# A decoder layer over 32 batches on one core: the loop body laid out anew on 20 slots, with the second score pass begun in a batch's own step

## The reference, cut to what matters

```python
# 1: self-attention whose small probabilities are cut
probs = softmax(x @ x.T * 256 ** -0.5)
vac = where(probs < 0.01, probs, 0).sum(-1)
sparse = where(probs < 0.01, 0, probs); sparse /= sparse.sum(-1) + 1e-9
x1 = layernorm(x + sparse @ x + 0.01 * broadcast(vac) @ W.T)
# 2: cross-attention, 16 heads of 16
q, k, v = x1 @ Wq + bq, ctx @ Wk + bk, ctx @ Wv + bv
x2 = layernorm(x1 + softmax(mask(q @ k.T / 4)) @ v @ Wo + bo)
# 3: a mixture of 8 experts, the best 2 by softmax(x2 @ Wr)
out = layernorm(x2 + sum of the two experts' (x2 @ Wi @ Wo) by their weights)
```

## Time and profile before

| | us |
|---|---|
| median of 3 runs (lowest, highest) | 911.61 (910.69, 917.72) |
| the profiled execution's own time | 906.62 |
| its span, first to last instruction | 904.5 |
| PE busy in the span | 809.0 (89%) |
| DVE busy | 691.5 (76%) |
| ACT busy | 614.2 (68%) |
| POOL busy | 200.0 (22%) |
| mean granted clock of PE, as a share of full speed | 0.982 |

### The profile page before, as it was taken

The page is one execution under the profiler, slowest core; times in us unless marked ns, Lnnn a source line. Parts: engine busy times, 40 slices in busy tenths (PEclk is TensorE's granted clock), DMA queues, the critical chain, the costliest instruction groups (busy, mean ns, idle before and its releaser), DMA issues.

```text
span 904.5 us, 22919 instructions
## 1 busy us (share of the span) xinstructions
PE 809.0 (89%) x7288; PEld 661.4 (73%) x7288; DVE 691.5 (76%) x2652; ACT 614.2 (68%) x1449; POOL 200.0 (22%) x293
## 2 busy tenths in 40 slices
PE   2768789999999999999999999999999999999875
PEld 2657667887777777787777777788777777777654
DVE  5445578888888888888888888888888888887745
ACT  1326677777877777777777777777887777777650
POOL 1201122222122222222222222222212222221011
PEclk9779999999999999999999999999999999999998
DMA  7354443444444444434444444343444444332100
GB/s 218 91 159 106 111 114 89 108 104 109 103 110 112 107 120 105 104 97 108 102 111 113 109 113 120 92 102 101 111 107 112 109 109 120 88 89 72 25 11 10
DMA packets 91159, 92.74 MB, mean 103 GB/s; under 512 B 16848, under 2 KB 86880, under 8 KB 91040
## 3 DMA queue, kind: packets, MB, share of 16 engines
q1 hardware_dynamic: 91040, 91.28, 39.6%
HBM read 28.44 MB, written 3.90 MB: 36 GB/s over the span
## 4 chain that ended last, share of the span: by engine, by line
PE 78%; ACT 6%; DVE 5%; SPq 5%; issue 4%; DMA 2%; POOL 0%; POOLq 0%; DVEq 0%; ACTq 0%
PE psum L1123 18%; PE psum L979 10%; PE psum L993 10%; PE psum L1009 9%; PE psum L1059 8%; PE psum L1052 7%; PE psum L1041 3%; PE psum L1081 3%; SPq L413 3%; ACT psum L515 2%; ACT probsT L526 2%; SPq L427 2%; PE psum L1069 1%; PE psum L1030 1%; PE psum L1023 1%
## 5 line engine op out<-in xcount | busy, mean ns | idle before, releaser
L672 DVE CUSTOM_DVE_ANT_0 scores_left<-psum,mask_add 112x375 f32<-112x375 f32 x512 | 278.3, 545 | 98.7 <-PE psum L979 90.3
L979 PE MATMUL psum<-k_stack,q_stack 96*112 96x376 f32 x512 | 196.6, 393 | 37.3 <-DVE nmax L672 23.7
L515 ACT ACTIVATE psum<-mask_u 125x448 f32<-125x448 uint8 x384 | 206.8, 543 | 10.2
L526 ACT ACTIVATE probsT<-psum 125x448 f32<-125x448 f32 x384 | 205.5, 535 | 4.2 <-PE psum L993 2.7
L993 PE MATMUL psum<-q_stack,k_stack 97*125 97x224 f32 x768 | 146.3, 279 | 11.2 <-ACT psum L515 10.9
L979 PEld LDWEIGHTS psum<-k_stack,q_stack 96*112 96x112 f32 x512 | 90.8, 177 | 80.0 <-issue 55.0
L993 PEld LDWEIGHTS psum<-q_stack,k_stack 97*125 97x125 f32 x768 | 130.2, 189 | 22.8 <-ACT psum L515 19.6
L686 DVE SCALAR_TENSOR_TENSOR mix<-psum,gate,mix 112x256 f32<-112x256 f32 x224 | 107.6, 480 | 17.0 <-PE psum L1123 4.7
L452 POOL TENSOR_SCALAR var_eps<-moments 112x1 f32<-112x1 f32 x96 | 21.2, 220 | 436.1 <-DVE moments L756 217.2
L1123 PE MATMUL psum<-we_hi,x_hi 128*112 128x512 f32 x256 | 107.4, 419 | 3.7 <-DVE mix L686 3.7
L488 POOL TENSOR_TENSOR ctx_lo<-ctx_sb,ctx_hi 128x752 fp32r<-128x752 f32 x32 | 57.2, 1789 | 202.3 <-DVE x_cas L812 202.3
(11 more groups left out here) (122 smaller groups left out, 1544.9 us busy)
## 6 DMA issues: line engine op xcount, KB each, us to landing
k_stack<-k_hi SPq DMA_DIRECT2D x256, 93.8 KB, 2.2
q_stack<-q_hi SPq DMA_DIRECT2D x256, 56.0 KB, 2.0
ctx_sb<-in_context_T SPq DMA_DIRECT2D x32, 376.0 KB, 3.3
k_stack<-k_lo SPq DMA_DIRECT2D x128, 93.8 KB, 2.2
q_stack<-q_lo SPq DMA_DIRECT2D x128, 56.0 KB, 2.0
xT<-in_x_T SPq DMA_DIRECT2D x32, 112.0 KB, 2.1
x_sb<-in_x SPq DMA_DIRECT2D x32, 112.0 KB, 2.2
out_dram<-out_sb SPq DMA_DIRECT2D x32, 112.0 KB, 2.8
```

The lines of the kernel that those rows point to most:

```text
L515: nc.scalar.activation(psum[0:KP, ST_BANKS[i % 2], 0:4 * TOK].rearrange("p (h q) -> p h q", h=4), mask_u8[b][:, KEYS + t * TOK:KEYS + (t + ...
L526: nc.scalar.activation(probsT[:, group % 2, t, :], psum[0:KP, ST_BANKS[i % 2], 0:4 * TOK], ACT.Exp, scale=-1.0).then_inc(probs_ready, 1)
L672: nc.vector.tensor_tensor_reduce(scores_left[:, n % 2, :], psum[0:TOK, S_BANKS[n % 2], 0:KEYS], mask_add[k][:, :], 1.0, 3.0e38, ALU.add, A ...
L979: nc.tensor.matmul(psum[0:TOK, S_BANKS[n % 2], 0:KEYS_EVEN], q_stack[b][0:96, c, pair, odd, :], k_stack[b][0:96, c, pair, :], start=True, ...
```

## The change

`USES` has new slots and banks, `moe` works on batch it-2 rather than it-3, and the last iteration is 34 rather than 35. The product with Wo, the norm and `x2T` (stage `join`) now belong to the iteration of `heads`; only the logits and the gate (`gate`, a new chain of semaphores) stand with `moe`.

```diff
-USES = [("x1T", 0, "G2"), ("m0", 1, "G1"), ("aT", 1, "G0"), ("qT", 2, "G2"), ("K0", 3, "G0"), ("Wo", 4, "G1"),
-        ("Sc", 5, "G2"), ("K1", 6, "G1"), ("m1", 8, "G0"), ("mx0", 8, "G2"), ("V0", 10, "G2"), ("x2T", 10, "G1"),
-        ("PT", 11, "G0"), ("m2", 12, "G2"), ("att", 13, "G1"), ("lg", 14, "G0"), ("V1", 15, "G2"), ("oT", 15, "O"),
-        ("m3", 16, "G1"), ("mx1", 16, "G0"), ("V2", 18, "G0")]
+USES = [("x1T", 0, "G2"), ("qT", 1, "G0"), ("lg", 2, "G1"), ("Sc", 3, "G0"), ("K0", 3, "G2"), ("m0", 4, "G1"),
+        ("mx0", 7, "G0"), ("K1", 7, "G2"), ("m1", 9, "G1"), ("oT", 10, "O"), ("V0", 10, "G0"), ("PT", 11, "G2"),
+        ("aT", 12, "G0"), ("att", 13, "G2"), ("m2", 13, "G1"), ("Wo", 14, "G0"), ("mx1", 14, "S1"), ("m3", 15, "G1"),
+        ("V1", 16, "G0"), ("V2", 18, "G0"), ("x2T", 19, "G1")]
...
-          "join": (-2, ("aT", "Wo", "x2T", "lg")),
-          "moe": (-3, ("m0", "m1", "m2", "m3")),
+          "join": (-1, ("aT", "Wo", "x2T")),
+          "gate": (-2, ("lg",)),
+          "moe": (-2, ("m0", "m1", "m2", "m3")),
```

On PE the scores of a batch's heads stand two slots earlier (heads 0 to 2 in slots 17 to 19 of the iteration before, the last in slot 12), and blocks 0 to 5 stand in slots 14 to 19 of the iteration in which the batch's maxima are taken, blocks 6 to 11 in slots 0 to 5 of the next:

```diff
-                    if attn and 0 < n < HEADS - 1:
-                        scores(a, n + 1)
-                    if n >= SLOTS - 2 and active("attn", it + 1):
-                        scores(p, n - (SLOTS - 2))
-                    if heads and n < BLOCKS - 1:
-                        score_block(w, n + 1)
-                    if n == SLOTS - 1 and active("heads", it + 1):
-                        score_block(a, 0)
+                    if attn and n + 3 < HEADS:
+                        scores(a, n + 3)
+                    if n >= SLOTS - 3 and active("attn", it + 1):
+                        scores(p, n - (SLOTS - 3))
+                    if heads and n + 6 < BLOCKS:
+                        score_block(w, n + 6)
+                    if attn and n >= 14:
+                        score_block(a, n - 14)
...
-                    if heads and n >= 4 and (n - 4) % 3 == 0 and n <= 13:
-                        weigh_values((n - 4) // 3)
+                    if heads and n in (2, 6, 8):
+                        weigh_values(w, (2, 6, 8).index(n) + 1)
+                    if attn and n == SLOTS - 1:
+                        weigh_values(a, 0)
```

```diff
 for n in range(SLOTS):
+    if moe and n == 0:
+        act.wait_ge(pe_join.sem, pe_join.to("x2T", o))
...
+    if heads and n + 5 < BLOCKS:
+        exponent(w, n + 5)
+    if attn and n >= 15:
+        exponent(a, n - 15)
     if proj and n == 0:
...
-    if heads and n < BLOCKS:
-        exponent(n)
-        if n + 2 < BLOCKS:
-            lay_mask(w, n + 2)
...
+    if heads and n + 7 < BLOCKS:
+        lay_mask(w, n + 7)
+    if attn and n >= 13:
+        lay_mask(a, n - 13)
```

More of the change, by code:

```diff
@@ L264, in decoder_layer @@
         pe_steps = {stage: Chain(sem(f"pe_{stage}"), [u for u, _, _ in ALL_USES if STAGE_OF[u] == stage])
-                    for stage in ("self", "proj", "attn", "heads", "join", "moe", "weights")}
+                    for stage in ("self", "proj", "attn", "heads", "join", "gate", "moe", "weights")}
         act_steps = {stage: Chain(sem(f"act_{stage}"), names) for stage, names in (
@@ L311, in stages @@
         def stages(it):
-            return [active(stage, it) for stage in ("self", "proj", "attn", "heads", "join", "moe")]
+            return [active(stage, it) for stage in ("self", "proj", "attn", "heads", "moe")]
         def batches(at):
-            return *[shift(at, ahead) for ahead in (2, 1, 0, -1, -2, -3)], at[1] % 2
+            return *[shift(at, ahead) for ahead in (2, 1, 0, -1, -2)], at[1] % 2
         block = ctx.enter_context(nc.Block())
@@ L373, in iteration @@
             def iteration(at, it):
-                own, proj, attn, heads, join, moe = stages(it)
-                s, p, a, w, o, m, k = batches(at)
-                if heads:
-                    neg_max_to_scratch(w, 1)
+                own, proj, attn, heads, moe = stages(it)
+                s, p, a, w, o, k = batches(at)
                 if active("self", it + 1):
@@ L410, in iteration @@
                     settle(sp)
-                    for n in range(PAIRS):
-                        for third, part in enumerate((q_hi, q_hi, q_lo)):
-                            sp.dma_start(q_stack[b][32 * third:32 * third + 32, :, n, :, :].bitcast(fp32),
-                                         part[32 * n:32 * n + 32, :, :, :].bitcast(fp32))\
-                                           .then_inc(q_stacked[b][n], 16)
+                    stack_queries(0)
+                    stack_queries(1)
                 if attn:
                     neg_max_to_scratch(a, 0)
+                if proj:
+                    stack_queries(2)
+                    stack_queries(3)
+                if attn:
+                    neg_max_to_stack(a, 0)
                 if proj:
@@ L422, in iteration @@
                     settle(sp)
[L423 to L431 removed]
+                    for n in range(PAIRS - 1):
+                        stack_keys(n)
+                if attn:
+                    neg_max_to_scratch(a, 1)
+                if proj:
+                    stack_keys(PAIRS - 1)
+                if attn:
+                    neg_max_to_stack(a, 1)
                 if it == FIRST:
@@ L576, in iteration @@
-                    if proj and n == 3:
+                    if proj and n == 2:
                         act.wait_ge(pe_proj.sem, pe_proj.to("qT", p))
@@ L786, in iteration @@
-                    if n == 10 and moe:
+                        if moe:
+                            dve.wait_ge(dve_gate.sem, dve_gate.to("gate_b", o))
+                            nc.vector.tensor_tensor(
+                                gate[k][:, :], gate_a[:, :], gate_b[:, :], ALU.add)\
+                              .then_inc(dve_gate.did("gate"), 1)
+                    if n == 8 and moe:
+                        expert(0)
+                        expert(1)
+                    if n == 9 and proj:
+                        low_keys(1)
```

508 lines of the change are left out of this document (252 added, 256 removed).

## The result

The changed kernel takes 997.38 us in the median of four runs (992.78 to 1009.3), the kernel before 911.31 beside it (910.69 to 917.72). The profiled execution, 1009.3 us with a span of 1007.3, lies 1.7% above the fastest and is left out of the comparison: the three others have a median of 993.62 us (992.78 to 1001.14), and the ratio is 1.091, 95% interval 1.0823 to 1.0997. The forecast was 950, at most 972. The mean granted clock is 0.930 in the profiled execution and 0.933 to 0.946 in the others.

A forecast was written before the change was run, and what follows sets the result against it. PE bounds the kernel now, SP's loop the changed one: 28 iterations of 27.0 us (756.0) plus front, partial iterations and end make 942.8 us of span, 944.9 with 2.1 around it, times 1.0055: 950 us, range 890 to 972.

The forecast's parts named there:

- the front: Start of the span: 46.5 us to batch 1's first `x1T`, next iteration 31.5, the first with `heads` 26.0.
- SP's loop: SP's copy queue, from `q_lo` to the last key copy needed before `x1T`: a period of 27.0 us, chance 0.50.
- the signs that it named for being wrong: No DMA wait ahead of `x1T`; `m1`, `m2` without gap; PE clock below 1.00 mid-run; end over 40 us after last maxima.
- The seam: Between two iterations on PE: block 7 starts 1.24 us after `x1T` instead of 1.81, a gain of 0.2 us.
- The loop through DVE and ACT: PE's waits at the seam, `m1`, `m2` and block 4 on 24.0 us of work: a period of 26.3 us.
- rival 4: PE's clock drawn to 0.9 by four gaps an iteration: 75 us more, a median over 1000; chance 0.02.
- One iteration less: Pipeline's end: 35.8 us after the last maxima instead of 47.1, gaining 11.3; one partial iteration (25.5) goes in front.
- The 19.5 behind it: From the last batch's `x2T` to the end: gate about 7, four products and sums 10.2, norm and output 2.3 us.

The follow-up runs named there:

- the kernel with the maxima's edit: Changed kernel, with ACT in slot 8 copying the first row of maxima ahead of `k_hi1`: 953.25 us, ratio 1.0468.
- E0: Not a run: one of the four products of the experts' weights on PE, which share a bank and wait for `we_lo`.
- E3, E1: Not a run: a product of the experts' weights on PE, moved by the change from bank G0 to G1.
- the kernel with POOL's copies: Changed kernel with mask behind its exponential, maxima before `k_hi1`, two experts' sums before head 14's maximum, last pair's key copies on POOL's queue: 914.34 us, ratio 1.003.
- the two fills: Unused matmuls ahead of products: five in iterations without attention (POOL copies, two weight products rebanked), 917.35 us; four in the last iteration (ACT copies), 919.05 us.
- its edit on ACT: Changed kernel, with each mask laid right behind its exponential on ACT, ahead of the slot's copies: 963.2 us, ratio 1.0567.
- late keys: Changed kernel with the first maxima ahead of `k_hi1`, and SP holding the last three key copies until block 4 of slot 18: 1091.73 us, ratio 1.1987.
- the old layout with late keys: Kernel before the change, with SP holding its last six key copies until the next batch's second score: 1022.68 us, ratio 1.1197.
- the kernel with ACT's queue: Changed kernel with mask behind its exponential, maxima before `k_hi1`, two experts' sums before head 14's maximum, last pair's key copies on ACT's queue: 919.99 us, ratio 1.0106.

## Why the prediction was wrong

It missed by 47 us in the median of the four runs, by 44 in that of the three others, and by 64 us of span in the profiled one (its terms add up to 943.3; the 942.8 is a slip, and so are 0.1 each in 4.9 + 0.81 = 5.8 and 24.4 + 2.2 = 26.5). The 64 are 37 for the clock, 12 for the front, 12 for the end and 6 for SP's loop, less 3 in between. Two of the signs that it named for being wrong came: a clock below 1.00 in the middle (0.95), and an end longer than 40 us (47.8). Step by step, for the span:

- **The seam**: right, block 7 at +1.24. **SP's loop**: right in each link at full clock: first query copy +5.9 (+5.9), SP goes on at +11.3 (+11.6), last key copy +24.4 (+24.2), period 27.0 (27.2 in the mean, 26.7 to 28.3). Over 28 iterations that is 6 us too little. The wait named as the one in SP's queue, for the first maxima behind `k_hi1`, was what made it the longest: the two lines exchanged ended that.
- **The loop through DVE and ACT**: right as a period, 26.3 (26.5 with SP's loop out of the way), though its waits were over-sized: 0.71, 0.42, 0.60 and 0.36 where it had 0.9, 0.7, 0.8 and 0.5, less 0.6. PE's own work, on the other hand, is 24.38 us in the iteration at full clock shown above, not 24.0. The two errors cancel, by luck.
- **The clock: the step that failed.** The text gave 0.02 to the rival that named it, and took no term for it, because "In the full iterations it is 1.00 in spite of a 0.84 us gap in each". That was an argument from one gap of 0.84 us, while the forecast itself put a second wait, for the key copy, 1 us in front of it. Ten iterations of 28 fell, 3.7 us each: 37 us. The sign was rival 4's, the size half of its 75. Its cause was only half right: not four gaps an iteration do it, since all four stay in the kernel with the maxima's edit at full clock, but the fifth, the wait for the key copy just ahead of the 0.71; with PE at work during that wait the falls went from 22 to two. What sets off a fall in one iteration and not in the next, with the same waits, stays open. The other executions fit: a mean clock of 0.946 in 990.7 and 991.5 us leaves 107 us at half clock, the 0.930 of the profiled one 141, and half of the difference, 17 us, is what they are shorter by; the third, 0.933 in 999.0 us, is 8 shorter where this gives 4. The Trainium skill's "TensorE: Matmul & The Clock Gate", section "A second HAM failure mode: psum-queue depth-cycling", says that short idling between groups can make the clock oscillate; the trace of the changed kernel agrees, with its ten falls behind pairs of 0.57 to 2.11 and 0.71 us.
- **The front**: 12 us over. Its first iteration took 26.2 and not 20.6 us, as the four products of the experts' weights (E0 to E3) share a bank and wait for `we_lo` (1.41, 0.39 and 0.60), and a mean clock of 0.8 came on top; the two after it took 5.7 more together. The change had moved E1 and E3 from bank G0 to G1 as well, and the prediction gives this no term. In the kernel with POOL's copies, bank G0 for the two took 1.6 us off the first iteration, but the next was longer by 4.2. Left open in its parts.
- **One iteration less**: wrong by 12 us; 47.8 from the last maxima to the end where 35.8 stood, so nothing was gained against 47.1 in the earlier trace rows. I took the last batch's `x2T` at +16.3; it stands at +25.3, as its norm is in DVE's slot 18 behind e6 and e7 of the batch before:

```profile
982.77 1.07 DVE L719 SCALAR_TENSOR_TENSOR mix<-psum,gate,mix 112x256 f32<-112x256 f32 x2 [0.62 <-PE psum L1150]
...
984.22 0.40 DVE L928 TENSOR_SCALAR x<-y,moments,rstd 112x256 f32<-112x256 f32 x1
...
994.62 1.07 DVE L719 SCALAR_TENSOR_TENSOR mix<-psum,gate,mix 112x256 f32<-112x256 f32 x2 [2.99 <-PE psum L1150]
```

The 19.5 behind it became 22.5, with the clock at 0.67: a product took 2.92 us and not 1.41 (the 2.99 is DVE's wait for it). 9 of the 12 us lie ahead of `x2T`, 3 behind it. Of the latter the two fills speak for the clock as the cause: the stretch got 4.2 and 3.8 us shorter with them, at a clock of 0.86 and 0.82, in one profiled execution each. That the former are the list of slots rests on these rows and on no run. From the last `x1T` to the last maxima it was 2.9 less than forecast.

What I would have needed was in my own text: a list of the waits with their places, not only their sum. Two of them stood side by side at the seam.

## What to carry to other kernels

Where PE is the bound, write down where its waits stand and how much work lies between them. A wait close ahead of another (here 0.57 to 2.11 us, 1 us of work, and 0.71 us) costs its length and may cost half of each microsecond that the clock then stays at half. So the first thing to remove is not the largest sum of waits but the wait that lets the clock fall, or else fill it with unused matmuls, if PE has no other work to do in it.

A queue of DMA issues is an engine. Here 24 copies at 0.64 us on SP closed a loop, and two exchanged lines on ACT, or three copies on another queue, were worth more (40 and 38 us) than any wait on PE (the 0.71 with its edit on ACT: 30); an edit that took a wait of 0.60 off PE elsewhere only made PE wait longer at the seam, and cost at least 34 us.

## What the runs showed of the hardware that I had not expected

- The clock falls with a PE that is 90% busy (720.46 of 798.80 us in the changed kernel). 1.56 us, more in some iterations, and 0.71 us of waiting at one place in 28 us brought 22 falls in 28 iterations; working through the first of the two brought it to 2. In the old layout one wait of 2.94 us in an iteration brought a fall in each.
- In the new layout a microsecond at half clock cost nearly half a microsecond: 78.5 us in the changed kernel against 10 x 3.7 = 37 us, 184.3 us with late keys against 28 x (31.3 - 28.1) = 90. In the old layout with late keys it was about a third: 150.2 us at half clock, against 28 x (29.1 - 27.3) = 50, where 27.3 is my estimate, as no iteration there ran at full clock.
- The three kernels with copies on POOL's queue went on for 5.8 us after their output had landed (the first: issued at 905.77, landed at 907.63, span 913.39), and the fourteen others for 0.5 (the changed kernel: 1004.98, 1006.83, 1007.31; the kernel with ACT's queue: 917.16, 919.02, 919.50). That cost, about 5.3 us once for the program, is more than the 3 us by which the kernel with POOL's copies trails the one before. A version ahead of both was not found: the best of the new layout is 914.34 us against 910.91.
